# Expert tiles of 128 rows, and the next tile's first product ahead of this tile's second

## The reference

```
x = x + attention(layernorm(x), ctx)
z = layernorm(x)
probs = softmax(z @ Wr.T);  top_v, top_i = top_k(probs, 2);  top_v /= sum(top_v)
for e in range(8):
    w_e = sum(where(top_i == e, top_v, 0))
    h = gelu(z @ W1[e].T + b1[e])          # 256 -> 1024
    out += (h @ W2[e].T + b2[e]) * w_e     # 1024 -> 256
x = x + out
```

## Time and profile before

| What | Value |
|---|---|
| Median of 3 runs | 479.6 us (478.82 to 484.76) |
| The profiled execution, timed | 480.8 us |
| Its span, first to last instruction | 478.9 us |
| TensorE busy | 411.0 us, 86% of the span |
| VectorE busy | 319.3 us, 67% |
| ScalarE busy | 198.8 us, 42% |
| GpSimd busy | 142.2 us, 30% |
| Mean granted TensorE clock | 0.944 |
| Chain that ended last: TensorE's share | 73% |
| First matmul of the expert stage | 211.8 us |

### The profile page before, as it was taken

The page is one execution under the profiler, slowest core; times in us unless marked ns, Lnnn a source line. Parts: engine busy times, 40 slices in busy tenths (PEclk is TensorE's granted clock), DMA queues, the critical chain, the costliest instruction groups (busy, mean ns, idle before and its releaser), DMA issues.

```text
span 478.9 us, 9857 instructions
## 1 busy us (share of the span) xinstructions
PE 411.0 (86%) x2876; PEld 317.9 (66%) x2877; DVE 319.3 (67%) x895; ACT 198.8 (42%) x339; POOL 142.2 (30%) x133
## 2 busy tenths in 40 slices
PE   3989899779898654039999999999999999999991
PEld 1345547436465543028888888888888888888880
DVE  2104755876769575917777777777777777777771
ACT  0214956775667464203443343333333434343330
POOL 8200300304253446800333222222223333222222
PEclk9999999999989975559999999999999999999997
DMA  7930037227534715240233332222222233332211
GB/s 241 327 117 0 22 117 247 90 88 237 203 121 130 258 65 167 78 144 1 46 50 67 53 53 44 46 44 44 44 44 44 44 49 62 56 54 44 44 22 23
DMA packets 32482, 43.46 MB, mean 91 GB/s; under 512 B 3088, under 2 KB 27920, under 8 KB 32336
## 3 DMA queue, kind: packets, MB, share of 16 engines
q1 hardware_dynamic: 19840, 27.24, 19.5%
q0 software_dynamic: 8880, 12.69, 13.8%
q10 hardware_dynamic: 3744, 3.31, 2.0%
HBM read 28.45 MB, written 14.78 MB: 90 GB/s over the span
## 4 chain that ended last, share of the span: by engine, by line
PE 73%; DVE 11%; ACT 4%; issue 4%; DMA 4%; POOL 2%; SPq 1%; POOLq 1%; DVEq 0%; ACTq 0%
PE o_ps L653 25%; PE s_ps L633 12%; PE t_ps L633 12%; PE proj L473 5%; PE s_ps L507 4%; PE o_ps L526 4%; PE proj L621 3%; PE proj L465 3%; DVE w2l L953 2%; PE proj L494 2%; POOL rows L404 2%; DMA xt<-rows 2%; PE proj L481 2%; PE t_ps L517 1%; DMA w2l<-ctxT 1%
## 5 line engine op out<-in xcount | busy, mean ns | idle before, releaser
L436 POOL DMA_INDIRECT out<-y,idx x46 | 72.5, 1576 | 196.7 <-DVE y L1189 189.7
L826 ACT ACTIVATE g<-s_ps,b_sb,down 128x256 f32<-128x256 f32 x92 | 46.9, 560 | 157.1 <-PE s_ps L633 157.1
L653 PE MATMUL o_ps<-w2h,gl 128*128 x368 | 100.3, 273 | 0.0
L653 PE MATMUL o_ps<-w2h,gh 128*128 x368 | 100.3, 273 | 0.0
L653 PE MATMUL o_ps<-w2l,gh 128*128 x368 | 100.3, 273 | 0.0
L1157 DVE TENSOR_SCALAR gh<-g,up 128x512 f16<-128x512 f32 x92 | 44.8, 486 | 40.9 <-ACT g L826 40.1
L1159 DVE SCALAR_TENSOR_TENSOR gl<-g,up,gh 128x512 f16<-128x512 f32 x92 | 69.1, 751 | 3.3
L826 ACT ACTIVATE g<-t_ps,b_sb,down 128x256 f32<-128x256 f32 x92 | 46.9, 559 | 13.5 <-PE t_ps L633 13.5
L404 POOL DMA_INDIRECT rows<-send,place x32 | 39.1, 1222 | 34.2 <-DVE place L1010 25.6
L653 PEld LDWEIGHTS o_ps<-w2l,gh 128*128 128x128 f16 x368 | 36.0, 98 | 4.2
L653 PEld LDWEIGHTS o_ps<-w2h,gl 128*128 128x128 f16 x368 | 36.0, 98 | 4.2
(11 more groups left out here) (160 smaller groups left out, 681.8 us busy)
## 6 DMA issues: line engine op xcount, KB each, us to landing
staged<-W1T SPq DMA_DIRECT2D x8, 1024.0 KB
staged<-W2T SPq DMA_DIRECT2D x8, 1024.0 KB
xt<-rows SPq DMA_DIRECT2D x23, 260.0 KB, 2.7
rows<-send POOLq DMA_DIRECT2D x8, 260.0 KB, 8.2
out<-x_sb ACTq DMA_DIRECT2D x4, 512.0 KB
w2l<-ctxT SPq DMA_DIRECT2D x4, 256.0 KB
x_sb<-x SPq DMA_DIRECT2D x2, 512.0 KB, 10.6
x_sb<-x ACTq DMA_DIRECT2D x2, 512.0 KB, 5.3
```

The source lines that it names most:

```text
L436: pool.indirect_dma_start(out=out, out_offset=bass.IndirectOffsetOnAxis(ap=idx[:, u, r:r + 1], axis=0), in_=y2[:, u, r, :], in_offset=None ...
L653: i = nc.tensor.matmul(y_ps[r][:, 0:D], l[:, m, r * P:(r + 1) * P], w[:, bass.ds(e, 1), m * D:(m + 1) * D].rearrange("p a n -> p (a n)"), ...
L826: i = nc.scalar.activation(g[:, m, :], h_ps[s][:, (m % MQ) * TR:(m % MQ + 1) * TR], ACT.Gelu, bias=b1_sb[:, bass.ds(e, 1), m:m + 1].rearra ...
```

## The change

The tile becomes 128 rows (TR = P), and there are (4096 + 8 x 127) // 128 = 39 of them. The four banks of the first product now hold two tiles of two halves each (`HALVES`), and every buffer between the two products is doubled (`g`, `xh`, `xl`, `gh`, `gl`). TensorE's order in tile t is: turn of t+2, first product of t+1, second product of t; VectorE's and ScalarE's orders follow. The ring `xt` has four slots of 128 rows. Repeated rows keep their own token's number but get a gate of zero (`fresh`), so `moved` and `idx` are gone: the scatter reads its indices straight from the slot of `xt`, and a slot is free when its scatter has landed.

```diff
-TR = 2 * P
+TR = P
-XR = 2
-QUARTERS = 4
+XR = 4
+HALVES = 2
...
-        xT_ps = proj[0]
+        xT_ps = proj
...
             def load_rows(t, slot):
                 if not isinstance(t, int) or t >= XR:
-                    sp.wait_ge(half_done, t * 2 - (2 * XR - 2))
+                    sp.wait_ge(added, t * 16 - (XR - 1) * 16)
...
-            def scatter(t, u):
+            def scatter(t, slot):
                 if not isinstance(t, int) or t:
-                    pool.wait_ge(added, t * 32)
-                for r in range(2):
-                    pool.wait_ge(y_ready, t * 2 + (r + 1))
-                    pool.sem_inc(half_done, 1)
-                    pool.indirect_dma_start(out=out, out_offset=bass.IndirectOffsetOnAxis(ap=idx[:, u, r:r + 1], axis=0),
-                                            in_=y2[:, u, r, :], in_offset=None, compute_op=ALU.add).then_inc(added, 16)
+                    pool.wait_ge(added, t * 16)
+                pool.wait_ge(y_ready, t + 1)
+                pool.sem_inc(scattering, 1)
+                pool.indirect_dma_start(out=out, out_offset=bass.IndirectOffsetOnAxis(ap=xt[:, slot, D + 3:D + 4].bitcast(I32), axis=0),
+                                        in_=y2[:, slot % 2, :], in_offset=None, compute_op=ALU.add).then_inc(added, 16)
...
-            def tile(t, nxt):
-                e = pe.value_load(expert_of[0:1, bass.ds(t, 1)], min_val=0, max_val=E - 1)
-                hidden(t, e)
-                if nxt is not None:
-                    turn_tile(t + 1, nxt)
-                second(t, e)
+            def tile(t, phase, ahead):
+                if ahead > 1:
+                    turn_tile(t + 2, (phase + 2) % XR)
+                if ahead > 0:
+                    hidden(t + 1, (phase + 1) % XR)
+                second(t, phase)
...
-                nc.vector.tensor_scalar(moved[:, 0, :], lane[:], again[:, bass.ds(t, 1)], None, ALU.is_lt).then_inc(marked, 1)
-                nc.vector.tensor_tensor(moved[:, 1, :], spare[:], token_no, ALU.subtract).then_inc(marked, 1)
...
+                nc.vector.scalar_tensor_tensor(out=gates[:, u, 2:3], in0=gates[:, u, 0:1], scalar=gates[:, u, 1:2],
+                                               in1=fresh[:, bass.ds(t, 1)], op0=ALU.add, op1=ALU.mult).then_inc(marked, 1)
...
+            def tile(t, phase, ahead):
+                if ahead > 1:
+                    take_tile(t + 2, phase % 2)
+                if ahead > 0:
+                    split(t + 1, (phase + 1) % 2)
+                mark(t, phase)
+                result(t, phase % 2)
```

More of the change, by code:

```diff
@@ L103, in build @@
         rank8 = sb("rank8", [P, QT, E])
-        token = sb("token", [P, NT])
-        lane = sb("lane", [P, 2])
-        spare = sb("spare", [P, 2])
+        token = sb("token", [P, NT], I32)
+        lane = sb("lane", [P, 1])
         b1_sb = sb("b1_sb", [P, E, MC])
@@ L636, in hidden @@
                             k += 1
-                    if m % MQ == MQ - 1:
+                    if m % MH == MH - 1:
                         i.then_inc(h_full, 1)
[L640 to L657, removed]
@@ L659, in tile, with second @@
-            def tile(t, nxt):
-                e = pe.value_load(expert_of[0:1, bass.ds(t, 1)], min_val=0, max_val=E - 1)
-                hidden(t, e)
-                if nxt is not None:
-                    turn_tile(t + 1, nxt)
-                second(t, e)
+            def second(t, slot):
+                e = pe.value_load(expert_of[0:1, bass.ds(t, 1)], min_val=0, max_val=E - 1)
+                if not isinstance(t, int) or t >= 2:
+                    pe.wait_ge(y_biased, t - 1)
+                for m in range(MC):
+                    if m % MH == 0:
+                        pe.wait_ge(gs_ready, t * HALVES + (m // MH + 1))
+                    for k, (l, w) in enumerate(((gh, w2h), (gh, w2l), (gl, w2h))):
+                        i = nc.tensor.matmul(y_ps[slot % 2][:, 0:D], l[:, slot % 2, m, :],
+                                             w[:, bass.ds(e, 1), m * D:(m + 1) * D].rearrange("p a n -> p (a n)"),
+                                             start=(m == 0 and k == 0), stop=(m == MC - 1 and k == 2))
+                i.then_inc(y_full, 1)
@@ L666, in _ @@
+            def tile(t, phase, ahead):
[4 more added lines that the diff above has]
+                second(t, phase)
             turn_tile(0, 0)
+            turn_tile(1, 1)
             pe.wait_ge(low_ready, UNITS)
[L668 to L672, removed]
@@ L673, in _ @@
-            tile(TILES - 1, None)
+            hidden(0, 0)
+            for t in range(3):
+                tile(t, t, 2)
+            with pe.Fori(3, TILES - 4, XR) as t:
+                for k in range(XR):
+                    tile(t + k, (3 + k) % XR, 2)
+            for t in range(TILES - 4, TILES):
+                tile(t, t % XR, min(2, TILES - 1 - t))
         @block.scalar
@@ L1162, in mark @@
[L1162 to L1168, removed]
+                for s in range(HALVES):
+                    dve.wait_ge(g_ready, t * HALVES + (s + 1))
+                    m = slice(s * MH, (s + 1) * MH)
+                    nc.vector.tensor_scalar(gh[:, u, m, :], g[:, u, m, :], by, None, ALU.mult).then_inc(g_high, 1)
+                    dve.wait_ge(g_high, t * HALVES + (s + 1))
+                    nc.vector.scalar_tensor_tensor(out=gl[:, u, m, :], in0=g[:, u, m, :], scalar=by, in1=gh[:, u, m, :],
+                                                   op0=ALU.mult, op1=ALU.subtract).then_inc(gs_ready, 1)
@@ L1169, in mark @@
+            def mark(t, slot):
+                u = slot % 2
+                first, second, choice = (xt[:, slot, D + k:D + k + 1] for k in range(3))
                 rank = rank_of[:, bass.ds(t, 1)]
-                nc.vector.scalar_tensor_tensor(out=gates[:, 0, :], in0=choice, scalar=rank, in1=first,
+                nc.vector.scalar_tensor_tensor(out=gates[:, u, 0:1], in0=choice, scalar=rank, in1=first,
                                                op0=ALU.is_equal, op1=ALU.mult).then_inc(marked, 1)
-                nc.vector.scalar_tensor_tensor(out=gates[:, 1, :], in0=choice, scalar=rank, in1=second,
+                nc.vector.scalar_tensor_tensor(out=gates[:, u, 1:2], in0=choice, scalar=rank, in1=second,
@@ L1178, in mark @@
[L1178 to L1185 removed]
+                dve.wait_ge(marked, t * 3 + 2)
@@ L1201, in _ @@
-            take_tile(0)
-            dve.wait_ge(b2_in, 16)
-            tile(0, 0, True)
-            tile(1, 1, True)
-            with dve.Fori(2, TILES - 2, 2) as t:
-                for k in range(2):
-                    tile(t + k, k, True)
-            tile(TILES - 1, 0, False)
+                if not isinstance(t, int) or t >= 2:
+                    dve.wait_ge(added, t * 16 - 16)
+                dve.wait_ge(y_biased, t + 1)
+                dve.wait_ge(marked, t * 3 + 3)
+                nc.vector.tensor_scalar(y2[:, u, :], y1[:, u, :], gates[:, u, 2:3], None, ALU.mult).then_inc(y_ready, 1)
@@ new lines, in tile @@
+            def tile(t, phase, ahead):
[5 more added lines that the diff above has]
+                result(t, phase % 2)
+            take_tile(0, 0)
+            take_tile(1, 1)
+            dve.wait_ge(b2_in, 16)
+            split(0, 0)
+            for t in range(3):
+                tile(t, t, 2)
+            with dve.Fori(3, TILES - 4, XR) as t:
+                for k in range(XR):
+                    tile(t + k, (3 + k) % XR, 2)
```

144 lines of the change are left out of this document (64 added, 80 removed).

## The result

The changed kernel takes 572.9 us (566.6 to 573.6, 4 runs) against 482.2 for the one before in the same job: 1.185 times its time, 95% interval 1.174 to 1.196. The forecast was 564, with a range of 528 to 593. The profiled execution spans 564.8 us. It is the fastest of six, at a mean granted clock of 0.949; four took 570.1 to 573.6 us at 0.919 to 0.923 and one 577.8 at 0.904, so some 6 us of the median stand in no trace.

A forecast was written before the change was run, and what follows sets the result against it. TensorE bounds the kernel before; after the change, the wait for scatter landing and reload sets the pace. First h at 215.6, 18 rounds x 17.8 = 320.4, then 27.1: span 563.1, timed 565.0, median 564 us, range 528 to 593.

The forecast's parts named there:

- The wait that the change adds: Expert stage: reloading a slot waits for tile t-4's scatter to land; chain of 16.4 us per round of two tiles.
- TensorE's own work: Expert stage: 2.62 + 2.62 + 0.33 = 5.6 us a tile, 39 tiles 217 us, 39 less than before.
- the clock: TensorE's clock falls to 1.2 GHz in most pauses, adding 1.4 us on average: 17.8 us a round of two tiles.
- the sign that the prediction set itself: TensorE waits for rows before the turn about 18 times, some 5 us each; wrong if absent or 1 us long.
- What bounds the kernel before: Expert stage: TensorE without a break, 109 ns a matmul of 256 columns, 11.1 us for each of 23 tiles.
- I take 54.6: TensorE's pitch for 128-column matmuls in ns, half of 109, if only columns count and weight loads overlap.
- h: Start of the first product in a round's first tile, from which the steps of the added wait are counted.
- five rounds of six: Share of rounds in which the cold clock costs 1.7 us in the first product, 1.4 on average.
- my second rival: The chain, with TensorE slower between matmuls by weight loads or register instructions; clock held at 98 ns, 580 us; chance 0.15.
- the main forecast: Expert stage: chain through scatter landing and reload, clock falling in most rounds, median 564 us; chance 0.55.
- VectorE's 5.3 us, costed at nothing: VectorE's splits, taking, mark, load and result, about 5.3 us a tile, hidden under 8.9.
- The other side: Rival: the ring hides the load, TensorE runs through, 443 us, VectorE's 5.3 us next; chance 0.05.

The follow-up runs named there:

- experiment 5: The kernel before with TensorE's weights at fixed addresses, always expert 0: 480.2 us against 480.2, ratio 0.999.
- experiment 8: The changed kernel with slots released once the scatter is begun, and fixed expert addresses on both TensorE and VectorE: 442.4 us, ratio 0.923 to the kernel before.
- experiment 2: The changed kernel with TensorE's weights at fixed addresses, always expert 0, slot release as in the change: 565.4 us, ratio 1.179 to the kernel before.
- experiment 3: The changed kernel with fixed weight addresses on TensorE and slots released once the scatter is begun: 469.4 us, ratio 0.975 to the kernel before.
- experiment 1: The changed kernel with token numbers copied out and slots released once the scatter is begun, not landed (early release): 528.1 us, 1.100 times the kernel before.
- experiment 7: The changed kernel with early release and the kernel before's order (first product of t, turn of t+1, second product of t): 572.7 us, ratio 1.193.
- experiment 10: The changed kernel with early release and fixed addresses in the second product alone, both expert-number loads kept: 490.7 us, ratio 1.015 to the kernel before.

## Why the prediction was right, and where it was not

The time was in the range, on the forecast side, and 9 us from the number. The wait that the change adds was named rightly, but two terms of the sum, TensorE's own work and the clock, were wrong and made up for each other; that the number came out so near is luck. By the sign that the prediction set itself (wrong if the pauses were absent or 1 us long) its picture of TensorE waiting 5 us in every round fails: from the fourth round on the pauses were under 1 us but for one.

**What bounds the kernel before**: right. TensorE, 109 ns a matmul; experiment 5 shows that its register instructions took nothing there.

**"I take 54.6"**: wrong as the changed kernel stands. The pitch was measured at 84 ns (4.04 us for 48) and a tile's own time at 8.5 us, not 5.6. I bounded the pitch by columns and by weight loads, and gave register instructions half a sentence in a rival. Weight loads were excluded for the right reason (the earlier trace rows have seven loads in the 0.26 us and not eight, which changes nothing): with fixed addresses it is 56 ns. The Trainium skill, "TensorE: Matmul & The Clock Gate", section Back-to-back issue gap, gives about 81 ns for sustained pairs; the 84 ns look like it, but in this kernel the weight load is not the cause, as the same pairs run at 56 ns in experiment 8. By the measurement its 81 ns is no floor.

**The wait that is added**: right in place and size. The steps, counted from h, in us:

| Up to | Forecast | Changed kernel | Fixed addresses (exp. 2) |
|---|---|---|---|
| last gelu ends | 5.0 | 5.7 | 6.2 |
| y1 starts | 7.4 | 8.25 | 8.7 |
| y2 ends | 8.3 | 9.3 | 9.9 |
| GpSimd starts | 8.8 | 10.1 | 10.7 |
| scatter landed | 12.5 | 13.9 | 14.4 |
| load issued | 13.6 | 14.7 | 15.2 |
| rows landed | 16.0 | 16.8 | 17.3 |
| next h | 16.4 | 17.65 | 17.9 |

The gelus end late for the slow matmuls in the one, for the slow clock in the other. Two steps were mis-sized in themselves. GpSimd starts 0.8 us after y2, though no second y2 follows, where I took 0.5 between the two readings of the earlier trace rows. And from landed rows to the next h it is 0.87 us, not 0.4, in the changed kernel: the turn takes 0.44, and 0.40 of "issue" follow it, in which TensorE loads the expert's number. The load's issue came 0.8 us after the landing and not 1.1, and the smaller load landed in 2.1, not 2.4.

**The clock**: wrong for the change, right for its premise. In the changed kernel it fell behind two pauses of 2.0 to 2.1 us at the start of the stage and then held, with pauses under 1 us and one of 1.2. In experiment 2 it fell behind all 18 pauses of 4.3 to 5.2 us; in the round shown it then stayed down for some 7 us, 4.5 of them with work. I had 3.4, which counts from the fall: in the stretch of the earlier trace rows work began again at 166.01 and the clock came back at 169.6, 3.6 later. My "five rounds of six" has no row behind it. A round took 17.9 there.

So the number was reached by another way. I had 1.4 us of cold clock in a round; in its place stand the slow first product, 0.7 up to the last gelu, and some 0.5 in the steps behind it. The pause of 5.3 us that I had is filled with TensorE's own slower work, which adds nothing to the round, since the round is set by the chain. It is my second rival ("TensorE slower between matmuls, by weight loads or by its register instructions", clock held, 580 us, 0.15) that describes this profile best, not the main forecast at 0.55. Its 580 were worked out from 98 ns a matmul.

**VectorE's 5.3 us, costed at nothing**: covered as said, but 0.8 short. Experiment 3 lays it bare at 6.1: register loads and waits between its operations were not in my sum, and some 0.2 us of it are the copy of the token numbers, which the change does not have.

**The other side** (443 us if the ring hides the load): experiment 1 removes the ring's wait and still gives 528, so this rival was worse than I wrote. Its number needs three things gone, and experiment 8, which takes away all three, gives 442.4.

Of the parts: tiles of 128 rows in the old order, with the early release, cost 93 us (572.7 against 480.2, experiment 7), the new order takes 45 back (experiment 1), and the late release costs 45 again (the change against experiment 1; 39 between the profiled executions). The size brings 15% fewer rows to compute (4992 for 5888), but each address in the weights, with its register instruction, now serves 128 rows in place of 256, and in the old order gelu and split stand in the chain.

## What to carry to other kernels

When a tile shrinks, count what a tile issues and not only what it computes: instructions that were covered by a long matmul become the pace, and they are added up over the whole tile, so a stretch with slack pays for one without. When a buffer is freed by something that must land, walk the whole way from the last reader to the next use and compare it with the time that the ring gives; here it was 9 to 11 us against one tile of TensorE's work. And an experiment that removes one of two limits of nearly the same size shows little (573 to 565): read its profile before saying that it did nothing.

## What the runs showed of the hardware

- A register instruction ahead of a matmul costs TensorE about 63 ns of supply (16 of them 1.0 us a tile, experiment 10), listed with 46 or 32 ns. In the kernel before, where all matmuls of a tile take 109 ns, 48 of them a tile cost nothing (experiment 5). In a tile that has short matmuls too, those of the long ones cost as well: experiment 10 removes just these.
- A single scatter starts 0.8 us after the operation that it waits for, in 37 of 39 tiles of the changed kernel (0.91 in the first; the last waited for a landing).
- In experiment 2 the clock fell to 1.2 GHz behind each of 18 pauses of 4.3 to 5.2 us, 2.1 to 4.9 us after the last matmul, 14 times before work began again. In the changed kernel it fell behind two of three pauses of 2.0 to 2.1 us, and behind none of the shorter ones, of up to 1.2 us.
